# Delta attention: VectorE transposes the block inverse, the output's squares ride in a later unit's statistics product, steps ordered anew

## What is computed

```
def _L0_attn_ref(hidden_states, ...):
    q = short_conv(x @ Wq.T, conv_q)      # 4 taps over time, then silu; k and v alike
    v_hat = k @ Wsv.T;  e = v_hat - v
    s = stack([sqrt(sum(e*e)), sum(|e|), 1 - cos(v_hat, v)])
    beta = sigmoid(mlp_b(s));  amp = mlp_a(s)
    g = -exp(A_log) * softplus(k / |k| * amp + dt_bias)
    def step(S, inp):                      # one token, state S is 128 x 128 per head
        S = S * exp(g_t)[..., None]
        delta = (v_t - k_t @ S) * b_t
        S = S + outer(k_t, delta)
        return S, (q_t * scale) @ S
    _, o = scan(step, S0, (qn, kn, v, g, beta))
    o = o * rsqrt(mean(o * o) + 1e-5) * norm_w * sigmoid(gate)
    return o @ Wo.T
```

## Time and profile before

| | us |
|---|---|
| median of three runs | 5595.47 |
| lowest, highest | 5595.19, 5602.07 |
| the profiled execution | 5594.32 |
| its span, first to last instruction | 5592.5 |
| the delta attention, about 36 to 2160 | 2124 |

### The profile page before, as it was taken

How to read it: one execution, slowest core, us unless ns; L and a number is a source line. 1 busy time by engine, 2 the same in 40 slices (tenths; PEclk the granted TensorE clock), 3 DMA queues, 4 the chain that set the end, 5 groups by cost and what they waited for, 6 DMA issues and landing times. The chain is left out here.

```text
span 5592.5 us, 159786 instructions
## 1 busy us (share of the span) xinstructions
PE 5352.9 (96%) x69266; PEld 3621.9 (65%) x69266; DVE 3326.5 (59%) x7451; ACT 2697.5 (48%) x5744; POOL 1898.1 (34%) x2352
## 2 busy tenths in 40 slices
PE   6999999999999998999999998999898999999999
PEld 3777777777777775677777754333365777667565
DVE  5888888888888884344444425766254444444222
ACT  5777677677777761355555521466611222222211
POOL 4888888878878881000000002000000111111000
PEclk9999999999999998999999998899999999999999
DMA  0000000000000000000000000000100111112100
GB/s 31 8 8 8 8 12 8 8 8 8 8 8 8 8 4 18 13 14 12 12 12 12 7 23 8 1 1 1 61 1 20 67 67 67 66 67 68 56 5 8
DMA packets 34300, 115.97 MB, mean 21 GB/s; under 512 B 4416, under 2 KB 9792, under 8 KB 33600
## 3 DMA queue, kind: packets, MB, share of 16 engines
q1 hardware_dynamic: 33600, 105.74, 5.4%
HBM read 103.63 MB, written 2.10 MB: 19 GB/s over the span
## 5 line engine op out<-in xcount | busy, mean ns | idle before, releaser
L700 POOL TENSOR_TENSOR d_kq<-d_kq,d_tot 128x512 f32<-128x512 f32 x448 | 526.6, 1175 | 43.7 <-PE d_lpd L324 43.7
L795 DVE SCALAR_TENSOR_TENSOR d_qkv<-d_fr,d_wts,d_qkv 128x509 f32<-128x509 f32 (+2 forms) x576 | 421.8, 741 | 25.0 <-ACT d_tail L573 21.4
L704 POOL TENSOR_TENSOR d_kF<-d_kF,d_tot 128x256 f32<-128x256 f32 x448 | 307.4, 686 | 274.0 <-PE d_lpd L318 264.6
L1975 DVE TENSOR_REDUCE r_nm<-r_ps 128x2 f32<-128x1024 f32 x256 | 307.8, 1222 | 142.5 <-PE r_ps L1794 142.3
L307 PE MATMUL d_fr<-xnT,d_wts 128*128 128x512 f32 x768 | 374.1, 610 | 6.7 <-DVE d_qkv L795 5.6
L1189 POOL TENSOR_TENSOR f1rstd<-f1var,mhalf 128x4 f32<-128x4 f32 x4 | 4.0, 1009 | 1090.3 <-DVE f1var L1214 1090.3
L2073 PE MATMUL e_pj<-xnT,e_wts 128*128 128x512 f32 x768 | 349.2, 604 | 12.7 <-DMA e_wts<-in_w3all 11.3
L1895 ACT ACTIVATE r_pT<-r_ps 128x512 f32<-128x512 f32 x512 | 274.9, 598 | 148.7 <-PE r_ps L1802 148.1
L1426 PEld LDWEIGHTS c_po<-c_pT,c_vt 128*128 128x128 f32 x2304 | 294.7, 191 | 21.0 <-ACT c_pT L1491 9.2
L1529 DVE TENSOR_TENSOR c_sc<-c_sc,c_mask 128x128 f32<-128x128 f32 x256 | 76.7, 300 | 382.8 <-PE c_sc L1381 382.8
L1426 PE MATMUL c_po<-c_pT,c_vt 128*128 128x128 f32 x2304 | 301.9, 276 | 0.2
(11 more groups left out here) (495 smaller groups left out, 13446.8 us busy)
## 6 DMA issues: line engine op xcount, KB each, us to landing
e_wts<-in_w3all SPq DMA_DIRECT2D x64, 897.0 KB, 4.5
d_wts<-in_headw SPq DMA_DIRECT2D x16, 583.5 KB, 3.8
c_wqo<-in_wqo SPq DMA_DIRECT2D x32, 256.0 KB, 2.6
f3ws<-in_f3w SPq DMA_DIRECT2D x17, 384.0 KB, 8.6
f2ws<-in_f2s SPq DMA_DIRECT2D x16, 256.0 KB, 6.2
f2qs<-in_f2q SPq DMA_DIRECT2D x16, 256.0 KB, 6.6
f1ws<-in_f1w SPq DMA_DIRECT2D x8, 384.0 KB, 6.1
f0ws<-in_f0w SPq DMA_DIRECT2D x6, 384.0 KB, 5.4
```

Source lines behind the costliest of these rows:

```text
L700: return nc.gpsimd.tensor_tensor(v, v, bc(bc(by_pair(u, lv)[:, :, 0], 2, h), 1, 2), ALU.mult)
L704: return nc.gpsimd.tensor_tensor(f, f, bc(by_pair(u, lv)[:, :, 1], 2, 1 << lv), ALU.mult)
L795: return nc.vector.scalar_tensor_tensor(into, fr[:, x // 2, 0:GRP - 3 + i], tap(u, x, i), into, ALU.mult, ALU.add)
L1975: nc.vector.tensor_reduce(nm[:, t % 2, half, 4 * j + i0:4 * j + i0 + 2], ps[:, row_pair(row - 1):row_pair(row - 1) + 2], AX, ALU.max).then ...
```

## The change

Five things, all inside `delta_attention`.

1. **Block inverse.** TensorE makes only `TB[:, 0]`'s orientation. The level-0 transposition with the identity goes, and so does, at levels 1 to 4, the product at column 2*P. VectorE subtracts on 128x128 instead of 128x256 and then transposes `TB[:, 0]` into `TB[:, 1]` in 32x32 blocks, once after level 0 and once after each of levels 1 to 4 (five transposes a unit).
2. **Squares of the output.** `osq` of an earlier unit becomes the eighth tile of a later unit's statistics product (row 1 of the fourth group), four units later (LAG = 4); `ms` is read from the same transposed bank as the statistics. The four one-column products stay only for the last four units. `og` becomes two buffers.
3. **Negated blocks.** The four operations that write `TT` and `Tm` from `xy` with a factor -1 move from VectorE to ScalarE.
4. **Offsets** are numbered anew (24 to 30 become 0 to 6).
5. **Order.** All four engines' bodies are written in another order.

The core of the diff:

```diff
-        osq, og = sb("osq", [P, GRP]), sb("og", [P, GRP])
+        osq, og = sb("osq", [P, GRP]), sb("og", [P, 2, GRP])
+        LAG = 4
...
@@ tensor
-                        in_blocks(0, low_b(0), eye_b, range(NB), 0, 0)
                         pe.wait_ge(scaled_kq[0], u + 1)
                         products(u, 1).then_inc(p_mm[1], 1)
...
-                        in_blocks(2 * P, Tb(0), Xb, range(NB), 0, 0)
-                        in_blocks(P, Xb, Tb(0), range(NB), 0, 0).then_inc(y_mm[2], 1)
+                        in_blocks(P, Xb, Tb(0), range(NB), 0, 0).then_inc(y_mm[2], 1)
...
-                        for j in range(7):
+                        for j in range(8):
                             r, e = j % 4, j // 4
-                            last = nc.tensor.matmul(fr[32 * r:32 * r + 32, 3, :], pick[:, e], sqs[:, j], start=(e == 0), stop=(e == 1 or r == 3),
+                            last = nc.tensor.matmul(fr[32 * r:32 * r + 32, 3, :], pick[:, e], sqs[:, j] if j < 7 else osq[:], start=(e == 0), stop=(e == 1),
...
+                        if u >= NU0 - LAG:
                             for j in range(NC):
                                 last = nc.tensor.matmul(fr[:, 2, j:j + 1], osq[:, ch_(j)], T.ones[:, 0:1], start=True, stop=True)
...
@@ scalar
+                        nc.scalar.activation(Tm[band(1)].rearrange("p (c r i) -> p c r i", c=NC, r=2)[:, :, 0], c3(xy[band(1), 2 * P:3 * P]), ACT.Copy, scale=-1.0)
+                        for r in (0, 2):
+                            last = nc.scalar.activation(TT[band(r), u % 2].rearrange("p (c r i) -> p c r i", c=NC, r=NB)[:, :, r + 1], c3(xy[band(r), P:2 * P]), ACT.Copy, scale=-1.0)
...
+                        nc.scalar.activation(odd(TT[0:64, u % 2], 64), mh(xy[0:64, 256:512], 64), ACT.Copy, scale=-1.0).then_inc(tt6_ready, 1)
...
@@ vector
-                        nc.vector.tensor_tensor(c3(TB[:, 1]), bc(eye[:], 1, NC), c3(xy[:, 0:P]), ALU.subtract).then_inc(tm0_ready, 1)
+                        nc.vector.transpose(TB[:, 1], TB[:, 0])
...
-                        dve.wait_ge(y_mm[4], u + 1)
-                        nc.vector.tensor_tensor(TB[:], TB[:], xy[:, P:3 * P].rearrange("p (x i) -> p x i", x=2), ALU.subtract).then_inc(tb_ready[4], 1)
+                        dve.wait_ge(y_mm[4], u + 1)
+                        ch.did(nc.vector.tensor_tensor(TB[:, 0], TB[:, 0], xy[:, P:2 * P], ALU.subtract), "tb_ready[4]", u)
+                        ch.after("tb_ready[4]", u)
+                        nc.vector.transpose(TB[:, 1], TB[:, 0]).then_inc(tm_ready[4], 1)
...
-                        nc.vector.scalar_tensor_tensor(ms[:], fr[:, 2, 0:NC], 1.0 / (P * P), eq[:, u % 4], ALU.mult, ALU.add).then_inc(ms_ready, 1)
+                        if u < NU0 - LAG:
+                            sv = fr[:, 3, :].rearrange("p (c r x) -> p r c x", c=NC, r=4)
+                            nc.vector.scalar_tensor_tensor(ms[:], sv[:, 3, :, 1], 1.0 / (P * P), eq[:, u % 4], ALU.mult, ALU.add).then_inc(ms_ready, 1)
```

More of the change, by code:

```diff
@@ new lines, in _ @@
+                    if (u := unit(t, 6)) is not None:
+                        if u >= NU0 - 3 and u + 1 >= NU0 - LAG:
+                            pe.wait_ge(ms_last, min(u + 1 + 1, NU0) - (NU0 - LAG))
+                        if u >= NU0 - 1 and u:
+                            pe.wait_ge(y_read[0], u)
+                        pe.wait_ge(diag_ready, min(u + 4, NU0))
+                        for j in range(NC):
+                            last = nc.tensor.matmul(fr[:, 2 + j // 2, (j % 2) * D:(j % 2 + 1) * D], og[:, u % 2, ch_(j)], wo[:, head(u) % 2], start=True, stop=True)
+                        last.then_inc(yo_mm, 1)
@@ L346, in _ @@
+                    if (u := unit(t, 1)) is not None:
+                        if u < 3:
+                            pe.wait_ge(round_v, u + 1)
+                        for j in range(NC):
+                            last = nc.tensor.transpose(fr[:, 0, ch_(j)], qkv[:, u % 3, 2, ch_(j)], T.ident[:])
+                        last.then_inc(vt_mm, 1)
+                    if (u := unit(t, 3)) is not None:
+                        pe.wait_ge(masked[2], u + 1)
                         in_blocks(0, low_b(2), Tb(1), range(NB), 0, 0).then_inc(x_mm[2], 1)
@@ new lines, in _ @@
+                    if (u := unit(t, 3)) is not None:
+                        pe.wait_ge(tm_ready[2], u + 1)
+                        in_blocks(0, low_b(3), Tb(1), range(NB), 0, 0).then_inc(x_mm[3], 1)
+                        pe.wait_ge(scaled_kq[4], u + 1)
+                        products(u, 5).then_inc(p_mm[5], 1)
+                    if (u := unit(t, 1)) is not None:
+                        pe.wait_ge(stat_read, u + 1)
+                        for j in range(NC):
+                            last = nc.tensor.transpose(fr[:, 3, ch_(j)], stat[:, ch_(j)], T.ident[:])
+                        last.then_inc(sT_mm, 1)
@@ new lines, in _ @@
+                    if (u := unit(t, 4)) is not None:
+                        if u >= NU0 - LAG:
+                            if u >= NU0 - 1:
+                                pe.wait_ge(osq_ready, u + 1)
+                            if u >= NU0 - 4:
+                                pe.wait_ge(kF_ready, min(u + 3, NU0))
+                            for j in range(NC):
+                                last = nc.tensor.matmul(fr[:, 2, j:j + 1], osq[:, ch_(j)], T.ones[:, 0:1], start=True, stop=True)
+                            last.then_inc(ss_mm, 1)
@@ new lines, in _ @@
+                    if (u := unit(t, 3)) is not None:
+                        pe.wait_ge(scaled_kF[6], u + 1)
+                        if u >= 2:
+                            pe.wait_ge(ms_ready, min(u - 2 + 1, NU0 - LAG))
+                        for j in range(NC):
+                            nc.tensor.transpose(fr[:, 3, ch_(j)], kF[:, u % 2, ch_(j)], T.ident[:])
+                        pe.wait_ge(xs_ready[6], u + 1)
+                        for j in range(NC):
+                            last = nc.tensor.matmul(xy[0:64, 256 + j * 64:256 + (j + 1) * 64], Xs[64:, j * 64:(j + 1) * 64],
+                                                    TT[64:, u % 2, j * P + 64:(j + 1) * P], start=True, stop=True, tile_position=(64, 0), skip_group_check=True)
+                        last.then_inc(yt_mm[6], 1)
@@ new lines, in _ @@
+                    if (u := unit(t, 2)) is not None:
+                        if u >= NU0 - 2 and u - 2 >= NU0 - LAG:
+                            pe.wait_ge(ms_last, u - 2 + 1 - (NU0 - LAG))
+                        if u < 3:
+                            pe.wait_ge(kF_ready, u + 1)
+                        for j in range(NC):
+                            for r in range(NB):
+                                last = nc.tensor.matmul(fr[band(r), 2, j * BW:(j + 1) * BW], kF[:, u % 2, blk(j, r)], qkv[:, u % 3, 0, blk(j, r)],
+                                                        start=True, stop=True, tile_position=(0, BW * r), skip_group_check=True)
+                        last.then_inc(dg_mm, 1)
+                        pe.wait_ge(kq1_ready, u + 1)
+                        products(u, 0).then_inc(p_mm[0], 1)
@@ L563, in _ @@
[L563 to L569 removed]
+                    if (u := unit(t, 0)) is not None:
@@ L609, in _ @@
-                    if (u := unit(t, 25)) is not None:
+                    if (u := unit(t, 1)) is not None:
                         if u == 0:
@@ L755, in _ @@
-                    if (u := unit(t, 28)) is not None:
                         scale_kq(u, 0).then_inc(scaled_kq[0], 1)
```

1027 lines of the change are left out of this document (503 added, 524 removed).

## The result

| | before | after |
|---|---|---|
| median, us | 5596.78 (4 runs) | 5456.69 (4 runs) |
| profiled execution, its span, us | 5594.3, 5592.5 | 5455.8, 5454.0 |
| ratio, 95% interval | | 0.9745, 0.9733 to 0.9757 |

140 us less, 2.5%. The forecast was 5493, its range 5432 to 5550: right in direction and inside the range, 36 us too slow.

The account below looks back on a forecast made before the run. The prediction took TensorE's work to bound the kernel: 2.50 - 0.5 - 0.5 - 0.2 + 0.3 = 1.6 us a unit, 102 us over 64 units, so 5493 us. The range was 5432 to 5550.

Parts of the forecast that it names:

- What bounds the kernel; what leaves TensorE: In the delta attention, TensorE's work and not its waits sets the pace; the pieces leaving it total 2.50 us a unit.
- The eighth product at 0: On TensorE, the added statistics product fills up the fourth round and costs 0; upper bound 0.9 us a unit.
- VectorE and ScalarE: VectorE loses 2.15 us, gains 1.4 (transposes 0.28 each), about 27.1 a unit; ScalarE gains 1.2 on some 23.
- The rule that the prediction quotes: VectorE's next operation waits until the pipe is empty, some 0.4 us a unit in all; the prediction said the trace disagrees.
- The slower rival: Transposes at 0.68 us make VectorE the bound: units 0.7 us longer, 5640 us, deciding from about 0.45; chance 0.09.
- Level 5: At this level of the inverse, products right behind X wait for ScalarE's copy: 0.5 us of TensorE's time.
- State of chunk 1, 0.5 us: TensorE's w of chunk 2 waits for this state behind VectorE's longer queue: 0.4 to 0.6, taken as 0.5 us.
- the longer chain: Subtract, transpose, then the next level's X: 0.3 us a level, costed at nothing; without cover 1.5 us a unit.
- GpSimd, 0.2: Level handovers through GpSimd cannot be shorter than 0.70 us; the loss is 0.2 us a unit, bounds 0 and 0.7.
- The pauses called issue: TensorE's waits marked issue, 14.1 us over 1000 us, part of about 0.8 us a unit; no gain counted for them.
- The wait at level 2, 0.3 back: TensorE's wait of up to 0.4 us for the copy of X of level 2 goes: 0.3 us a unit regained.
- Fill left alone: Pipeline fill and drain taken as unchanged: same depth, fewer products, one transpose more in each link.

Follow-up runs that it names:

- a_seven: The changed kernel without the eighth statistics product, so the output's squares are not summed: 5464.4 us, against 5464.5 for the changed kernel on these chips.
- The first part alone: The kernel before, in its own order, with only the block-inverse change (TensorE pieces out, five VectorE transposes in): 5532.3 us, ratio 0.9854 to the kernel before.
- a_best: The changed kernel with rb's transposes behind X of level 5, VectorE's MLP product later, GpSimd's level-0 scaling earlier, ScalarE's MLP silu later: 5572.6 us, ratio 0.9928.

## Right and wrong, step by step

- **What bounds the kernel; what leaves TensorE: right.** TensorE's busy time fell from 31.3 to 28.5 us a unit (974.9 of 1000 us in 31.2 units, 956.0 in 33.6), 2.8 for the 2.50 of the sum. Put back, the column sums cost their 0.93, and the other pieces 1.2 of 1.58.
- **The eighth product at 0: right**, by the rows and by a_seven.
- **VectorE and ScalarE: right.** 26.5 us a unit for 27.1, transposes at 0.30 for 0.28, ScalarE 23.8 where it had 22.7, about the 1.2 that were added. For VectorE's sum there is luck in it: the polynomial and the MLP's last step lost 0.7 and 0.6 us of being held up, and the MLP's product, the level-0 difference and two more gained 0.2 to 0.3 each, none of it foreseen. The rule that the prediction quotes from the Trainium skill (VectorE: DVE Perf Modes, The DRAIN you can't avoid) ends there with an exception, which the prediction left out: "A next op that is not held starts earlier". The rows fit the exception: the transpose at 663.02 lasts 0.30 and the mask behind it starts at 663.25, 0.23 later. The slower rival, VectorE as the bound, was far from its point: five more operations cost nothing. (Its point of 0.45 us a transpose goes by a unit of 31.1 us, its time by one of 31.7, with which the point would be 0.55.)
- **Level 5: right place**, 0.38 us for 0.5.
- **State of chunk 1, 0.5 us: wrong.** No such wait exists. The step that failed is the price of the MLP's 128x4 operation: I took the earlier trace rows's 852 ns for its own cost and carried it to its new place. It takes 0.22 there, and those 0.63 are more than the whole wait of 0.5. Its shortest case in the kernel before was 0.20 already:

```profile
L830 DVE TENSOR_SCALAR d_bx<-d_ba,d_mb x64: 199/866/874, 78.3 to 2087.5; 128x4 f32<-128x4 f32 x64
```

The 0.87 of the kernel before was GpSimd's: the row below starts 0.30 us behind GpSimd's scaling and ends when GpSimd goes on to its next one.

```profile
648.83 0.87 DVE L830 TENSOR_SCALAR d_bx<-d_ba,d_mb 128x4 f32<-128x4 f32 x1
```
```profile
648.53 1.15 POOL L700 TENSOR_TENSOR d_kq<-d_kq,d_tot 128x512 f32<-128x512 f32 x1
649.63 0.29 POOL L709 TENSOR_TENSOR d_tot<-d_tot 128x64 f32<-128x64 f32 x1
```

- **The mask of level 1: not foreseen**, 0.45 us a unit. I had costed the longer chain at nothing in the new order; what made it late is a meeting with GpSimd, at L1052.
- **GpSimd, 0.2: 0.33** (11.2 us in 33.6 units), at level 0, within the bounds. My own terms (0.03, 0.20 and about as much at level 0) add up to some 0.45, and I put down 0.2. Its waits at level 1 are the 0.74 that I expected; at level 2 they are 0.64 in one half of the units and 1.28 in the other, where I had 0.8, and 0.64 is less than the 0.70 that I took for the least.
- **The pauses called issue: missed.** They were in the rows (14.1 us, 0.45 a unit), and I left them in the sum. They vanished; why is open (last section).
- **The wait at level 2, 0.3 back: right**; it is gone.
- **Fill left alone: wrong by 9 us.** In the new order the first K projection stands ahead of the four banks of the gate's product instead of behind them; v_hat of the first unit starts at 48.4 instead of 57.3. The first part alone does not have this (56.2).

In sum: of the 36 us the start is 9, and the rest is that 63 distances fell by 2.07 us each and not by 1.6. In the middle of the stage, which the waits can be read for, a unit fell by 2.3 (32.1 to 29.8), 0.7 more than I had. Of these 0.4 are waits: I had them grow by 0.9 us a unit and they grew by 0.5 (1000 - 974.9 in 31.2 units, 0.81; 1000 - 956.0 in 33.6, 1.31). The other 0.3 are TensorE's busy time, which no run takes apart. The first five distances, where the pipeline fills, fell by only about 1.5 us in all, which brings the mean down. So the time came out near through misses both ways: the state's 0.5 and the pauses' 0.45 were not lost, and the mask's 0.45 was.

## What to carry to other kernels

On an engine that is busy 96% of its time, removed work is worth nearly its full price even when several new waits come with it; sum the pieces, then look for waits. Before an operation's duration is carried to a new place, look at its shortest case and at what GpSimd does beside it: a 128x4 step at 0.85 us is no slow step but a held-up one. When an activation is moved ahead of another, see whose wait the table load then hides behind. And where TensorE's waits grow, look at its granted clock: in a_best the slower matmuls cost more than the waits.
